# An output projection moved from the tiles of tokens to the heads, with scatters that add to DRAM

## The reference, cut to what matters

```
h = layernorm(x) * (1 + ca) + sa                      # x: 4 x 2048 x 512
Q, K, V = h @ Wq.T + bq, h @ Wk.T + bk, h @ Wv.T + bv  # 16 heads of 32
top = the 409 queries of the largest norm, for each of the 64 (batch, head) pairs
out_sel = softmax(Q[top] @ K.T / sqrt(32)) @ V
out = zeros; out[top] = out_sel                        # rows not chosen stay zero
x = x + ga * (out @ Wo.T + bo)
h = layernorm(x) * (1 + cb) + sb
q = fp4 quantise and dequantise in blocks of 16
x = x + gb * (q(silu(q(h) @ q(Wg).T) * (q(h) @ q(Wu).T)) @ q(Wd).T)   # hidden width 1408
```

## Time and profile before

| | |
|---|---|
| median of 3 runs | 3258.67 us (3257.95 to 3259.64) |
| the profiled execution | 3256.89 us, its span 3255.0 us |
| PE busy | 3148.5 us, 97% of the span |
| DVE, POOL, ACT busy | 2545.4, 1563.1 and 1141.7 us |

### The profile page before, as it was taken

One profiled execution on the slowest core, in us unless ns is written; L12 is line 12 of the kernel. 1 busy time (PEld: TensorE's weight loads), 2 busy tenths in 40 slices (PEclk: granted clock), 3 DMA queues, 4 the chain that ended last, 5 costly groups with the idle time before them and its releaser, 6 DMA issues.

```text
span 3255.0 us, 49640 instructions
## 1 busy us (share of the span) xinstructions
PE 3148.5 (97%) x16552; PEld 1459.3 (45%) x16552; DVE 2545.4 (78%) x3750; ACT 1141.7 (35%) x1588; POOL 1563.1 (48%) x1420
## 2 busy tenths in 40 slices
PE   7999999799999999999999999999999999999998
PEld 3543454333333333333455555555555555555554
DVE  4658976566666666666799989889999998899985
ACT  6853333366666666665211111111111111111111
POOL 3432224356666666663544444444444444444442
PEclk9999999899999999999999999999999999999999
DMA  6858849854333333324100010000000010000000
GB/s 237 285 174 250 220 137 251 204 174 142 86 103 106 86 116 95 84 78 126 42 30 30 29 32 32 29 31 30 29 29 29 32 32 29 30 31 29 29 20 17
DMA packets 238230, 290.81 MB, mean 89 GB/s; under 512 B 94648, under 2 KB 150328, under 8 KB 237384
## 3 DMA queue, kind: packets, MB, share of 16 engines
...
...
## 4 chain that ended last, share of the span: by engine, by line
PE 74%; ACT 2%; DVE 2%; issue 1%; POOL 1%; DMA 0%; SPq 0%; ACTq 0%; POOLq 0%; DVEq 0%
PE bank L1625 12%; PE pair L2158 9%; PE pair L2160 9%; PE pair L2159 9%; PE pair L1614 7%; PE pair L1576 5%; PE bank L2182 4%; PE bank L2180 4%; PE bank L2181 4%; ACT shared L1517 2%; PE pair L2137 2%; PE pair L2138 2%; PE pair L2139 2%; PE bank L2170 1%; PE pair L2170 1%
## 5 line engine op out<-in xcount | busy, mean ns | idle before, releaser
L1412 DVE TENSOR_REDUCE top<-pair 128x1 f32<-128x1024 f32 x378 | 451.0, 1221 | 219.2 <-PE pair L1576 219.2
L1517 ACT ACTIVATE shared<-pair,p_bias 128x820 f32<-128x820 f32 x512 | 483.3, 944 | 373.8 <-PE pair L1614 373.6
L2158 PE MATMUL pair<-gu,xT_hi 128*128 128x512 f16 (+1 forms) x1536 | 555.9, 362 | 4.1 <-DVE bridge L1919 2.1
L2160 PE MATMUL pair<-gu,xT_lo 128*128 128x512 f16 (+1 forms) x1536 | 555.8, 362 | 0.0
L2159 PE MATMUL pair<-gu,xT_hi 128*128 128x512 f16 (+1 forms) x1536 | 555.7, 362 | 0.0
L1625 PE MATMUL bank<-shared,bridge 128*33 128x410 f32 x2048 | 404.2, 516 | 0.0
L455 POOL DMA_INDIRECT q_sel<-q_d,chosen x256 | 247.3, 966 | 96.7 <-issue 80.6
L1614 PE MATMUL pair<-q_exp,bridge 98*128 98x410 f16 x1024 | 267.8, 343 | 25.9 <-ACT shared L1517 25.4
L1373 POOL DMA_INDIRECT o_d<-o_rows,chosen x256 | 250.1, 977 | 81.5 <-issue 64.2
L2180 PE MATMUL bank<-dn,bridge 128*128 128x512 f16 x704 | 268.4, 381 | 0.0
L2181 PE MATMUL bank<-dn,bridge 128*128 128x512 f16 x704 | 268.2, 381 | 0.0
...
## 6 DMA issues: line engine op xcount, KB each, us to landing
bridge<-k_d SPq DMA_DIRECT2D x384, 128.0 KB
v_d<-v SPq DMA_DIRECT2D x16, 1056.0 KB, 10.0
...
```

The source lines that it names most:

```text
L1412: ve.tensor_reduce(top[:, t, half:half + 1], ps[:, :, :].rearrange("p a n -> p (a n)"), AX.X, ALU.max, negate=True).then_inc(max_done, 1)
L1517: act.activation(p32[k % PB][:, :, :], ps_exp[:, :, 0:NQ], ACT.Exp, bias=con["p_bias"][:, 0:1], scale=scale).then_inc(p_done, 1)
L2158: pe.matmul(o, xT_hi[:, c, :], w_hi[:, c, c0:c0 + n], start=c == 0, stop=False)
L2160: last = pe.matmul(o, xT_lo[:, c, :], w_hi[:, c, c0:c0 + n], start=False, stop=c == KC - 1)
```

## The change

The projection with Wo leaves the feed forward stage. Each head's divided rows are now cut in halves (DVE), turned back by PE (`turn_back`, four small matmuls), copied to SBUF as float16 (`take_back`, DVE) and multiplied with the 32 rows of Wo that belong to the head: `project`, one matmul for each of the four tiles of queries, 96 rows deep since the three products of halves lie above one another, 512 columns wide. A table `PROJECT_AT` puts the four at steps 5 and 7 of the slot two heads on, and 1 and 3 of the slot three heads on. ACT takes tiles 0 and 2 out of PSUM, DVE tiles 1 and 3 (`take_rows`). POOL scatters them with indirect DMAs that add (`compute_op=ALU.add`) to whole rows of 512 numbers in `o`, which is now filled with the bias `bo`. The taken tiles lie in two sets of four buffers, in the space of the down weights, which are therefore loaded when all heads are stored. The first scatter of a head waits for all scatters of the head before.

In the feed forward stage `attention_out`, `turn_a`, `high_of_a`, `low_of_a` and `take_attention` are gone; `residual` reads the tile of `o` as it was loaded. `turn_x` of tile t+1 moves into `down(t-2)`, and `low_of_x` to the end of DVE's slot. Of the hidden quantisation, the step that scales the exponent goes to ACT (`magic`), and the masking of the exponent (`bitwise_and`) moves to the end of `hidden_units`. The scale of a block is made with `scalar_tensor_tensor` and a constant tile `least` in place of `tensor_scalar`. The handoff of the last heads is written anew (`last`): projections of heads 61 to 63 stand between the three `gate_up` of tile 0.

The diff, cut to its core:

```diff
+    BACK_AT = 2
+    PROJECT_AT = {5: (-2, 0, False), 7: (-2, 1, True), 1: (-3, 2, True), 3: (-3, 3, False)}
     CHUNKS_AT = {0: ((1, 3), (1, 4)), 2: ((1, 5), (1, 6)), 4: ((2, 0),), 6: ((2, 1), (2, 2))}
...
+                def load_wo(h):
+                    need(sp, o_proj, (h - 1) * QT)
+                    c, at = h % H // QT, h % QT * HD
+                    for k, part in enumerate((0, 0, 1)):
+                        sp.dma_start(wo_head[h % 2][k * HD:(k + 1) * HD, :], wo[part][at:at + HD, c, :]).then_inc(wo_in[h % 2], 16)
+
...
+                    part, w = divmod(k, 2)
+                    sp.dma_start(ffn["gu"][part][w][:, :, :], scratch["gu"][part, w]).then_inc(con["f_in"], 16)
+
+                def load_bv(h):
+                    need(sp, o_cut, h - 1)
+                    sp.dma_start(bv_head[h % 2][:, :], early["bv"][:, h % H * HD:(h % H + 1) * HD]).then_inc(bv_in[h % 2], 16)
...
-                        sp.dma_start(o_blocks[b + 1, j // 2], zeros[:, :].unsqueeze(1).to_broadcast([P, TB, D])).then_inc(o_zeroed, 16)
+                        sp.dma_start(o_blocks[b + 1, j // 2], bo[:, :].unsqueeze(1).to_broadcast([P, TB, D])).then_inc(o_zeroed, 16)
...
+                    load_bv(i)
+                    if i >= 1:
+                        load_wo(i - 1)
...
                 def scatter(h):
-                    u = h % 2
-                    pool.wait_ge(o_divided, h + 1)
-                    pool.tensor_tensor(o_rows_of[u][:, :, :], o_rows_of[u][:, :, :],
-                                       early["bv"][:, h % H * HD:(h % H + 1) * HD].unsqueeze(1).to_broadcast([P, QT, HD]),
-                                       ALU.add).then_inc(o_biased, 1)
-                    pool.wait_ge(o_biased, h + 1)
-                    if h % H == 0:
-                        pool.wait_ge(o_zeroed, 16 * (L // N) * (h // H + 1))
                     for t in range(QT):
...
-                        pool.indirect_dma_start(o_rows, bass.IndirectOffsetOnAxis(ap=con["chosen"][0:n, t, h:h + 1], axis=0),
-                                                o_rows_of[u][0:n, t, :], None).then_inc(o_stored[u], 16)
-
+                        pool.wait_ge(o_taken[t % 2], h * 2 + t // 2 + 1)
+                        if t == 0:
+                            for k in range(QT):
+                                need(pool, o_stored[k], 16 * h)
+                            if h % H == 0:
+                                pool.wait_ge(o_zeroed, 16 * (L // N) * (h // H + 1))
+                        pool.indirect_dma_start(o_rows, bass.IndirectOffsetOnAxis(ap=token[0:n, t, h:h + 1], axis=0),
+                                                o_tile[h % 2][t][0:n, :], None, compute_op=ALU.add).then_inc(o_stored[t], 16)
...
+                def take_rows(h, u, t, bank):
+                    n = rows_of(t, TOP)
+                    ve.wait_ge(o_proj, h * QT + t + 1)
+                    need(ve, o_stored[t], h * 16 - 16)
+                    ve.tensor_scalar(o_tile[u][t][0:n, :], bank[0:n, :], 1.0 / (W_UP * O_UP), None, ALU.mult).then_inc(o_taken[1], 1)
+
+                def take_back(h, u, bank):
+                    ve.wait_ge(o_back, h + 1)
+                    need(ve, o_proj, h * QT - QT)
+                    ve.tensor_copy(oT[u][:, :], bank[0:KROWS, 0:NQ]).then_inc(o_back_taken, 1)
+
...
-                    ve.wait_ge(o_step, h * 3 + 3)
-                    need(ve, o_stored[u], stored)
-                    ve.tensor_tensor(o_rows_of[u][:, :, :], o_both[:, :, 0:HD],
+                    ve.wait_ge(o_step, h * 5 + 3)
+                    need(ve, o_cut, h)
+                    ve.tensor_tensor(o_div[:, :, :], o_both[:, :, 0:HD],
                                      o_inv[:, :].unsqueeze(2).to_broadcast([P, QT, HD]), ALU.mult).then_inc(o_divided, 1)
...
+                    ve.wait_ge(o_divided, h + 1)
+                    ve.wait_ge(bv_in[u], loaded)
+                    ve.tensor_tensor(o_div[:, :, :], o_div[:, :, :], bv_head[u][:, :].unsqueeze(1).to_broadcast([P, QT, HD]),
+                                     ALU.add).then_inc(o_step, 1)
+                    ve.wait_ge(o_step, h * 5 + 4)
+                    need(ve, o_back, h)
+                    ve.tensor_copy(o_split[:, :, :].rearrange("p t (k r) -> p t k r", k=3)[:, :, 0:3:2, :],
+                                   o_div[:, :, :].unsqueeze(2).to_broadcast([P, QT, 2, HD])).then_inc(o_step, 1)
+                    ve.wait_ge(o_step, h * 5 + 5)
+                    ve.tensor_tensor(o_split[:, :, HD:2 * HD], o_div[:, :, :], o_split[:, :, 0:HD], ALU.subtract).then_inc(o_cut, 1)
...
+                def take_rows(h, u, t, bank):
+                    n = rows_of(t, TOP)
+                    act.wait_ge(o_proj, h * QT + t + 1)
+                    need(act, o_stored[t], h * 16 - 16)
+                    act.activation(o_tile[u][t][0:n, :], bank[0:n, :], ACT.Copy, scale=1.0 / (W_UP * O_UP)).then_inc(o_taken[0], 1)
...
+                            d, t, misc = PROJECT_AT[k]
+                            if t % 2 == 0 and has(i, d):
+                                take_rows(i + d, (u + d) % 2, t, ps_misc if misc else ps_max[1 - u][:, 1, :])
...
+                def turn_back(h, bank, by, taken):
+                    pe.wait_ge(o_cut, h + 1)
+                    need(pe, o_taken[by], taken)
+                    for t in range(QT):
+                        n = rows_of(t)
+                        last = pe.matmul(bank[0:KROWS, t * P:t * P + n], o_split[0:n, t, :], con["ident16"][0:n, 0:n],
+                                         start=True, stop=True)
+                    last.then_inc(o_back, 1)
...
+                def project(h, u, t, bank, loaded, by, taken):
+                    n = rows_of(t, TOP)
+                    if t == 0:
+                        pe.wait_ge(wo_in[u], loaded * 3)
+                        pe.wait_ge(o_back_taken, h + 1)
+                    need(pe, o_taken[by], taken)
+                    pe.matmul(bank[0:n, :], oT[u][:, t * P:t * P + n], wo_head[u][:, :], start=True, stop=True).then_inc(o_proj, 1)
...
-                            for c in (STEPS - 2, STEPS - 1):
-                                weigh(i - 1, 1 - u, c, None)
+                            weigh(i - 1, 1 - u, STEPS - 2, None)
+                            project_in_turn(i, u, k)
+                            weigh(i - 1, 1 - u, STEPS - 1, None)
                         elif k > 1 and k % 2 == 1:
-                            for c in (k - 3, k - 2):
-                                weigh(i, u, c, in_turn(i, u, 0))
-                        if k == QUERIES_AT and has(i, 2):
-                            turn_queries(i + 2, u)
+                            if k < STEPS - 1:
+                                project_in_turn(i, u, k)
+                            weigh(i, u, k - 3, in_turn(i, u, 0))
+                            if k == STEPS - 1:
+                                project_in_turn(i, u, k)
+                            weigh(i, u, k - 2, in_turn(i, u, 0))
                         if k == GATHER_AT and has(i, 1):
                             gather_last(i + 1)
                         if k == ROWS_AT and has(i, 1):
                             rows(i + 1)
-                        for d, c in CHUNKS_AT.get(k, ()):
+                        for n, (d, c) in enumerate(CHUNKS_AT.get(k, ())):
                             if has(i, d):
                                 scores_for_max(i + d, (u + d) % 2, c, in_turn(i, u, d))
...
+                        if k == BACK_AT and has(i, -2):
+                            turn_back(i - 2, ps_misc, 0, (i - 3) * 2 + 2)
                         if k == TURN_AT and has(i, -1):
...
-        ve.tensor_scalar(sc[:, :], am[:, :], 1.0 / 6.0, 1e-12, ALU.mult, ALU.max).then_inc(step, 1)
+        ve.scalar_tensor_tensor(out=sc[:, :], in0=am[:, :], scalar=1.0 / 6.0, in1=least[:, 0:nb], op0=ALU.mult,
+                                op1=ALU.max).then_inc(step, 1)
...
         def hidden_units(t):
             ve.wait_ge(hid_done, t * NG + NG)
-            block_units(ve, t, FF, hid, am2, sc2, in2, xn2, q2_step, lambda: need(ve, q2_done, t))
+            block_units(ve, t, FF, hid, am2, sc2, in2, xn2, q2_step, lambda: need(ve, q2_done, t), -1.0)
+            ve.wait_ge(q2_step, t * QS + 4)
+            ve.tensor_scalar(mg2[:, :].bitcast(I32), xn2[:, :].bitcast(I32), EXP_BITS, None, ALU.bitwise_and).then_inc(q2_step, 1)
...
-            add_magic(ve, t, xn2, mg2, q2_step)
+            ve.wait_ge(q2_step, t * QS + 6)
+            ve.scalar_tensor_tensor(out=xn2[:, :], in0=mg2[:, :], scalar=ROUND, in1=xn2[:, :], op0=ALU.max, op1=ALU.add)\
+              .then_inc(q2_step, 1)
...
-            take_magic(ve, t, xn2, mg2, q2_step, q2_round)
+            ve.wait_ge(q2_step, t * QS + QS)
+            ve.scalar_tensor_tensor(out=xn2[:, :], in0=mg2[:, :], scalar=ROUND, in1=xn2[:, :], op0=ALU.max, op1=ALU.subtract)\
+              .then_inc(q2_round, 1)
...
-            else:
-                low_of_x(t)
```

(35 more changed lines are left out.)

268 lines of the change are left out of this document (140 added, 128 removed).

## The result

The changed kernel takes 3305.45 us (3302.98 to 3307.60, 4 runs) where the kernel before takes 3259.01: 1.0143 of it, interval 1.0125 to 1.016. It is 46 us slower. A second set of runs gave 3308.0 against 3257.24, 1.0155 (1.0138 to 1.0172).

What follows compares the result with a forecast made beforehand. PE was taken to bound the heads, and a chain through DVE and POOL the changed tiles. 3256.9 + 72 (heads) - 56 (tiles) - 6 (transition) - 1 (end) = 3265.9 us, 3267 as a median; range 3190 to 3320 us.

Steps and rivals of the forecast that it cites:

- the likeliest case: Whole kernel: the forecast of 3267 us itself, with its own range 3240 to 3295 us and chance 0.47.
- rival 4: Heads: PE's new waits on DVE's copies and PSUM banks make a head 1.9 us longer, 3310 us; chance 0.15.
- The closed chain: Tiles: a path through DVE and POOL from one scale of 32 blocks to the next sets the tile, 25.13 us.
- the one between 1.26 and 2.80 for the sum: Tiles: POOL's sum, held up by hidden_add, taken as 2.55 us between no meeting (1.26) and a full one (2.80).
- the lock on the scale: Tiles: DVE's scale of 32 blocks, 1.83 us, waits for POOL's product of 1408 columns, in both forms.
- Rivals 1 and 2: Tiles: PE stays the bound, 23.0 to 23.3 us, chance 0.11; or the scale's swap helps, 24.4 us, chance 0.18.
- PE's own work a tile: Tiles: PE's work without attention_out and turn_a, 26.05 - 3.03 = 23.02 us.
- Rival 1: Tiles: ports don't bind and PE stays the bound, -165 to -179 us, 3150 to 3160 us; chance 0.11.
- I take 0.18 for both: Heads: PE's price for splitting weigh by float16 matmuls twice, between nothing and 0.16 us for each.
- rival 3: Heads: the adding scatters bind, 17.1 us of DMA over the 15.5 of a head, about 3363 us; chance 0.09.
- I take -6 us, bounds -9 and +6: Transition: 12 us of PE's projections and turns leave, ten projections, two turn_back and waits come.
- 977 ns each as now: Heads, POOL: each scatter was taken to cost POOL the same as in the kernel before.

Runs made afterwards that it cites:

- e2: Changed kernel with the block maxima and the reciprocals of the scales in a free PSUM bank from tile 5 on; 3224.35 us, 0.9899 of the kernel before.
- e5: Changed kernel with POOL making the product of tile t+2 at the end of its slot; 3351.72 us on another chip, 1.0173 of the kernel before there.
- e3: Changed kernel with the scale of a block made by tensor_scalar again, without the tile least; 3302.40 us, 1.0133 of the kernel before.
- e11: Changed kernel with the edits of e1, e2 and e5 and the transition of e10 together; 3182.49 us, 0.9768 of the kernel before.
- e1: Changed kernel with all four projections of a head between scores and weigh, none inside weigh; 3285.81 us, 1.0086 of the kernel before.
- e4: Changed kernel with scatters that write instead of add, leaving out the sum over the heads; 3296.26 us, 1.0118 of the kernel before.
- e6: Changed kernel, tile 2's input scaled before the last eight scatters, tile 3's loaded before SyncE's wait; 3412.38 us on another chip, 1.0373 of the kernel before.
- e10: Changed kernel, tile 2's input and tile 0's hidden values scaled between the last two heads' scatters, tile 3's input loaded early; 3305.52 us, 1.0145 of the kernel before.
- e9: The changed kernel again, unaltered, beside the kernel before; 3308.00 us, 1.0155 of the kernel before.

## Why the prediction was right in sign and short in size

The range of 3190 to 3320 us holds the time and the side is right, but the forecast of 3267 lies 38 us low, and the likeliest case's own range of 3240 to 3295 misses it. By the table of stages the miss is 41 us on the profiles: 23 us of the transition, 14 of the heads and 4 of the stretch ahead of them. That the range holds the time is in part luck: it reaches that high for rival 4, waits in the heads, at 3310 us, and these did not come.

**The tiles: right, in mechanism and size.** Forecast 25.1 us and -56, measured 25.11 and -55.3. The closed chain can be walked in the tile shown above: end of L1901 2511.94 to the end of L1906 2520.22, 8.28 (8.24 forecast); masking, `low_of_x` and `take_down` to 2522.35, 2.13 (2.16); result, product and sum 2497.13 to 2502.42, 5.29 (1.35 + 1.35 + 2.55 = 5.25), the moments to the end of L1901 9.52 (9.48). Of the choices, the one between 1.26 and 2.80 for the sum was 2.55, and 2.55 it is (2499.87 to 2502.42). The four parts of this tile come to 25.22, which is its own length (2496.45 to 2521.67). That the lock on the scale is in the chain was only argued from rows 5 to 8; e2 shows it, together with what else it moves to PSUM; e5 shows that POOL's stretch is in it too, e3 that both forms of the scale are held. In the 13 tiles where the clock was low the chain runs through the late activation instead, which the prediction didn't have. Rivals 1 and 2 are out for this kernel; e2 and e11 bring their conditions about. PE's own work a tile was put at 23.02 us, and e11 shows 23.24 (23.43 less 0.19 idle). Rival 1's own sum comes to 3143 to 3157 us, not 3150 to 3160.

**The heads: mechanism right, one term too small.** "I take 0.18 for both" was the price of splitting `weigh` twice, on top of the projections' own 0.216 each. It measured 2 x (0.45 - 0.216) = 0.47, above the bound of 0.16 for each; e1 gets back 0.35 of it by placing both ahead of `weigh`. The projection at step 3 takes 0.33 us where 0.22 was counted, 0.11 more; why it differs from the one at step 5 is open. `turn_back` less the idle time is 0.00 and not 0.05, and the waits are nothing and not 0.1. Forecast 1.2 us a head, measured 1.45: +85.7 us in place of +72. No wait on `o_taken` or the banks showed, so rival 4 is out, and rival 3 as well: the DMA share is 0.72 (its own case, 11.3 of 15.5 us, is 0.73), and e4 takes the adding away without moving the period.

**The transition: wrong.** "I take -6 us, bounds -9 and +6" failed, in the step that counts PE's work and leaves the queues out. PE's busy time did fall, 102.3 to 101.1 us, part of it at the lower clock; its idle time grew from 10.3 to 28.5. The sum had no term for POOL's queue, in which 16 scatters in place of eight stand between the first tiles' work, nor for their price, 1.57 us and not "977 ns each as now". By idle time e4 shows that the adding, by its issue and by the wait for its landing, makes 5 to 7 us of the 18: it has 22.5, where the five profiles of the unaltered transition have 27.8 to 29.3. e6 and e10 show that moving POOL's scalings alone doesn't mend it, since the next wait stands close behind. Of the rest, two waits stand behind DVE and stay in e4, e6 and e10 too: 4.26 us for `oT` (none in the kernel before) and 4.44 for `xT_lo` (1.88 before). What they would leave if they went was not run. The lower clock that follows such waits comes on top: with the same idle time PE's busy time was 101.0 us in the first profile and 107.1 in e9.

**What is not explained.** The gap of 3.8 us in ACT on one chip. The heads of e6 took 101 us more there than the same heads in e10, and the kernel before took 34 us more in all. No profile of the kernel before exists from that chip. And it is open why the same transition got 0.86 of the clock in one profile and 0.93 in another.
